# Moving two token mixes of the second batch into the first batch's tail, and its attention front to earlier places in the first FFN

## The chip, the cores and the metric

One core of a Trainium2 chip runs the kernel. The metric is the device time of one execution in microseconds (us), as the median of several runs. The engines are TensorE (PE in the profile, with its weight loads as PEld), VectorE (DVE), ScalarE (ACT), GpSimd (POOL) and SyncE (SP), which issues the DMAs.

## The reference

The input holds 8 batches of 512 tokens. Three layers follow one another; the last two add to their input.

```python
h = jnp.einsum('bhid,oi,od->bho', x, weighted_sum, weight)       # token mix, 1024 -> 256
h = h + attention(layernorm(h))    # qkv, rotate, unit q and k, 16 heads of 16, softmax, out projection
h = h + ffn(layernorm(h))
# ffn: 8 experts, 256 -> 1024 -> 256
w = sigmoid(x @ Wg + bg); w = w * (w > 0.5)
out = sum_e w[:, e] * (relu(x @ W1[e] + b1[e]) @ W2[e] + b2[e])
```

## The kernel before

Each batch has four tiles of 128 tokens. The kernel overlaps the FFN of batch i with the attention of batch i+1. The order is written out as a list of stages, which every engine walks in the same sequence, each doing its own part of a stage and waiting on semaphores. `attention_order` gives every stage a due time, counted in chunks of the FFN; `bodies` merges them with the FFN's stages. There are 64 chunks (8 experts x 8); chunk c has a first matmul `f1 c` (6 matmuls of 512 columns) and, three chunks later, a second `f2 c` (12 matmuls of 256 columns), and after each eighth `f2` comes `acc e`, in which VectorE adds the expert's result to the output tile.

There are four orders: the first (attention of batch 0 alone, then `f1 0` to `f1 3`), the second (FFN of batch 0 beside attention of batch 1), the merged one (six times), and the last. Only the first two are touched here. The stages of an attention are:

- `split t`: ScalarE rounds tile t of the input to its high part (`xh`), and VectorE subtracts for the low part (`xl`), each in two halves.
- `mix t`: TensorE makes the token mix in 24 matmuls of 256 columns (12 for each half of the input), VectorE copies the result to `resid` and takes its statistics (`bn_stats`).
- `ln1`: a chain of small VectorE instructions for the inverse root, then the four normalised tiles.
- `ln1_turn t`, `qkv t`, `rotate t`: transposes, the projection (12 matmuls), then VectorE's work on the rotary part. Then `qk_norm`, `unit t`, `stack t` (ScalarE high part, VectorE low part of q and k), and SP's DMA transposes.
- `scores`, `weigh`, `out_copy`, `out_turn`, and then the tail: `att_turn t`, `project t`, `ln2`, `ln2_turn t`, `logits t`, `gates`, `gates_turn`, `bias2`.

During the second order, the weights of the experts 2 to 7 are also prepared: `maxima 2e` and `maxima 2e+1` search the raw W1 and W2 of expert e on VectorE (one reduction of 128x2048 each), `share e` is a tiny matmul that spreads the maxima over the partitions, `scales e` makes the factors, and `parts 4e` to `parts 4e+3` split the weights (ScalarE high, VectorE low). SP loads the next raw W1 once parts 4e+1 is done, and the next raw W2 once parts 4e+3 is done. So `load_raw` of expert 4 waits for the parts of expert 3.

In the second order GpSimd makes the low part of each hidden chunk (`hl`), and `f2 c` waits for it. The TensorE stage `f1 n` waits for ScalarE's two activations of chunk n-2, since the two banks `bank_h` alternate. The relevant waits in the code are:

```python
elif stage == "f1":                       # TensorE
    wait(pe, h_hi, fb, 2 * (n - 1))
elif stage == "f2":
    wait(pe, h_lo, fb, n + 1)
    ...
        if m == 0 and t % 2 == 0:
            wait(pe, acc_done, fb, TT * (e - 1) + t + 2)
```

Before the change the first order ends with `ln2, ln2_turn, logits, gates, split_ahead 0, f1 0, f1 1, f1 2, gates_turn 0, f1 3, bias2 0`, and the second order opens with `maxima 5, f2 0, split 1, mix 0, f1 4, split 2, mix 1, share 2, f2 1, scales 2, f1 5, split 3, mix 2, f2 2, f1 6, mix 3, f2 3, ln1, f1 7, f2 4, ln1_turn 0, f1 8`. `maxima 4` stands between `scores 28` and `scores 29` of the first order.

## Time and profile before

| | us |
|---|---|
| median of 3 runs | 1892.27 (1889.27 to 1893.55) |
| the profiled execution | 1891.92 |
| its span in the trace | 1890.1 |
| TensorE busy in the span | 1813.9 |
| VectorE busy | 1312.3 |
| ScalarE busy | 1076.7 |

The trace has no marks by batch; by the bias adds of `bias2` (at 128.57 and 370.39 us) the first order ends at about 128.5 us and the second some 10 us after 370. Times below are microseconds from the span's start. A row of the timeline gives start, duration, engine, line, operation and operands; square brackets at its end give the idle time of the engine just before it and who ended that. TensorE's matmul records overlap, so a matmul's pace is the distance between starts and not its duration.

### The profile page before, as it was taken

The numbers are of one execution on the slowest core, as the hardware profiler recorded it, in microseconds if no ns is written. First come the engines' busy times: TensorE is split into PE (matmuls) and PEld (weight loads), VectorE is DVE, ScalarE is ACT, GpSimd is POOL, SyncE is SP. The second block draws the span as 40 slices with busy tenths as digits, with TensorE's granted clock in tenths as the row PEclk, the third lists the DMA queues.
The fourth block names the chain that finished last, engine by engine and source line by source line (L and its number), as shares of the span: only waits on it lengthen the run. The fifth ranks groups of instructions, "written<-read, shape, count | busy, mean of one in ns | idle before, by whom it ended". The sixth has DMA issues, their size and how long they took to land.

```text
span 1890.1 us, 33337 instructions
## 1 busy us (share of the span) xinstructions
PE 1813.9 (96%) x13036; PEld 1173.0 (62%) x13036; DVE 1312.3 (69%) x2469; ACT 1076.7 (57%) x1658; POOL 111.6 (6%) x92
## 2 busy tenths in 40 slices
PE   5689899999999999999999999999999999999999
PEld 4157445775567655776557755677556775566666
DVE  7868645688865888558875788758886588863333
ACT  3745777446654566446664466544765456654444
POOL 1013323200000000000000000000000000000000
PEclk9789999999999999999999999999999999999999
DMA  4332552415122331234312242221512323223221
GB/s 166 112 112 90 147 180 99 168 51 151 69 89 101 84 140 68 69 121 113 112 68 90 79 134 90 89 98 71 156 68 70 121 70 111 89 72 117 92 104 42
DMA packets 103979, 192.40 MB, mean 102 GB/s; under 512 B 67448, under 2 KB 80656, under 8 KB 87440
## 3 DMA queue, kind: packets, MB, share of 16 engines
q1 hardware_dynamic: 103824, 190.28, 30.5%
q8 instruction: 104, 1.70, 0.4%
q14 instruction: 51, 0.42, 0.1%
HBM read 153.55 MB, written 20.97 MB: 92 GB/s over the span
## 4 chain that ended last, share of the span: by engine, by line
PE 81%; DVE 5%; issue 3%; ACT 3%; DMA 2%; DVEq 0%; ACTq 0%; SPq 0%
PE bank_h L1069 32%; PE bank_f L1088 11%; PE bank_f L1090 10%; PE bank_f L1091 10%; PE bank_o L975 4%; PE bank_s L950 4%; PE bank_s L855 3%; PE bank_s L856 3%; PE bank_s L857 3%; DMA qt<-probs 2%; ACT hh L832 1%; PE bank_m L987 1%; PE bank_s L1023 1%; PE bank_m L864 1%; PE bank_o L864 1%
## 5 line engine op out<-in xcount | busy, mean ns | idle before, releaser
L1069 PE MATMUL bank_h<-x,w1s 128*128 128x512 f16 x3072 | 749.7, 381 | 2.4 <-ACT hh L832 2.4
L829 ACT ACTIVATE h<-bank_h,b1s 128x512 f32<-128x512 f32 x512 | 352.2, 688 | 539.9 <-PE bank_h L1069 470.3
L1088 PE MATMUL bank_f<-w2s,hh 128*128 128x256 f16 x2048 | 560.2, 274 | 6.0 <-DVE acc L1362 5.9
L1090 PE MATMUL bank_f<-w2s,hh 128*128 128x256 f16 x2048 | 558.4, 273 | 0.0
L1091 PE MATMUL bank_f<-w2s,hl 128*128 128x256 f16 x2048 | 558.3, 273 | 0.0
L1069 PEld LDWEIGHTS bank_h<-x,w1s 128*128 128x128 f16 x3072 | 289.3, 99 | 296.2 <-issue 23.2
L1144 DVE TENSOR_TENSOR hl<-h,hh 128x512 f16<-128x512 f32 x448 | 309.9, 695 | 136.6 <-PE bank_f L1091 107.0
L832 ACT ACTIVATE hh<-bank_h,b1s 128x512 f16<-128x512 f32 x512 | 349.7, 683 | 0.0
L1088 PEld LDWEIGHTS bank_f<-w2s,hh 128*128 128x128 f16 x2048 | 201.3, 98 | 106.9 <-issue 48.0
L1090 PEld LDWEIGHTS bank_f<-w2s,hh 128*128 128x128 f16 x2048 | 200.6, 98 | 49.7 <-issue 0.3
L1091 PEld LDWEIGHTS bank_f<-w2s,hl 128*128 128x128 f16 x2048 | 200.4, 98 | 23.3
L798 ACT ACTIVATE qk<-bank_s 128x1024 f32<-128x1024 f32 x132 | 135.3, 1025 | 64.3 <-PE bank_s L950 64.2
L1283 DVE TENSOR_TENSOR probs<-qk,probs 128x1024 f16<-128x1024 f32 x132 | 161.8, 1225 | 4.5
L1362 DVE SCALAR_TENSOR_TENSOR acc<-bank_f,gw,acc 128x256 f32<-128x256 f32 x256 | 106.1, 477 | 38.1 <-PE bank_f L1091 37.1
L1282 DVE CAST probs<-qk 128x1024 f16<-128x1024 f32 x132 | 91.1, 690 | 51.9 <-ACT qk L798 51.8
L975 PE MATMUL bank_o<-probs,v 128*32 128x512 f16 (+1 forms) x1408 | 115.3, 427 | 1.0 <-ACT tmp_b L727 0.6
L950 PE MATMUL bank_s<-qt,kt 64*128 64x512 f16 x480 | 94.2, 389 | 15.8 <-DMA qt<-w1s 4.7
L707 POOL TENSOR_TENSOR resid<-resid,outb 128x1024 f32<-128x1024 f32 x8 | 25.4, 3170 | 1135.2 <-DVE normed L1195 1128.5
L680 POOL TENSOR_TENSOR hl<-h,hh 128x512 f16<-128x512 f32 x64 | 76.6, 1196 | 198.5 <-ACT hh L832 148.4
L855 PE MATMUL bank_s<-mix,xh 128*128 128x256 f32 x240 | 73.0, 304 | 14.1 <-DVE xl L1135 12.6
L950 PEld LDWEIGHTS bank_s<-qt,kt 64*128 64x128 f16 x480 | 23.1, 92 | 98.3 <-issue 58.3
L798 ACT ACTIVATE stack<-bank_s 128x1024 f32<-128x1024 f32 x60 | 61.5, 1026 | 37.1 <-PE bank_s L950 37.1
(215 smaller groups left out, 1800.2 us busy)
## 6 DMA issues: line engine op xcount, KB each, us to landing
w1s<-w_parts SPq DMA_DIRECT2D x56, 1024.0 KB, 4.8
w2s<-w_parts SPq DMA_DIRECT2D x56, 1024.0 KB, 4.8
raw<-in_w_dram SPq DMA_DIRECT2D x16, 1024.0 KB, 6.3
xraw<-in_x_t_dram SPq DMA_DIRECT2D x30, 512.0 KB, 6.1
w_parts<-w1s SPq DMA_DIRECT2D x8, 1024.0 KB, 8.8
w_parts<-w2s SPq DMA_DIRECT2D x8, 1024.0 KB, 10.6
out_dram<-acc SPq DMA_DIRECT2D x16, 256.0 KB, 6.0
w1s<-in_x_t_dram SPq DMA_DIRECT2D x2, 512.0 KB, 9.0
```

Source lines behind the costliest of these rows:

```text
L798: act.activation(terms, score_banks(n, fb is None)[:, :, :], ACT.Exp, scale=SCORE_SCALE)\
L829: act.activation(h32[n % 2][:], bank_h[n % 2][:, :], ACT.Relu, bias=b1s[:, e, m:m + 1]).then_inc(h_hi.sem, 1)
L832: act.activation(hh[n % HBUFS][:], bank_h[n % 2][:, :], ACT.Relu, bias=b1s[:, e, m:m + 1]).then_inc(h_hi.sem, 1)
L855: pe.matmul(out_ap, high[k], w[k], start=start and k == 0, stop=False, skip_group_check=True)
L950: pe.matmul(score_banks(n, fb is None)[:, j, :], kt[lo:lo + 64, h // 2, tile * P:(tile + 1) * P], qt[lo:lo + 64, h // 2, :], start=True, s ...
L975: last = pe.matmul(bank_o[32 * j:32 * j + 32, :], v[:, 4 * g + j].rearrange("p s d -> p (s d)"), p[:, j, :], start=(tile == 0 and k == 0), ...
L1069: last = pe.matmul(bank_h[n % 2][:, :], w[:, wp, k, m * P:(m + 1) * P], x16s[fb % 2][:, xp, k, :], start=(k == 0 and wp + xp == 0), stop=( ...
L1088: pe.matmul(o, high, w[:, 0, m, :], start=(m == 0 and t % 2 == 0), stop=False, skip_group_check=True)
L1090: pe.matmul(o, high, w[:, 1, m, :], start=False, stop=False, skip_group_check=True)
L1091: last = pe.matmul(o, low, w[:, 0, m, :], start=False, stop=(m == HM - 1), skip_group_check=True)
L1144: dve.tensor_tensor(hl[n % HBUFS][:], h32[n % 2][:], hh[n % HBUFS][:], ALU.subtract)\
L1283: dve.tensor_tensor(low, exps[n % 3], high, ALU.subtract).then_inc(halved.sem, 1)
```

## The change

Stages of the second batch move, and some change their engine or bank:

- `maxima 4` leaves the scores of the first order and stands at the head of the second.
- `split_ahead 0` (tile 0 of batch 1) goes from just ahead of `f1 0` up to just ahead of `weigh 15`.
- `mix_early 0` to `3` are the two tile mixes 0 and 1 in half tiles of 12 matmuls, in `bank_h` in place of `bank_s`. The first stands between `out_turn 3` and `att_turn 0`, the second between `att_turn 1` and `project 0`, the third and fourth between `project 3` and `ln2`.
- `split_early 0`, `1` split tile 1, the low part on GpSimd in place of VectorE. `resid_early` copies the mix on ScalarE in place of VectorE, and `stats_early` takes its statistics on VectorE, among the `ln2_turn` stages.
- `split_ahead 2` stands where `split_ahead 0` stood.
- In the second order `mix 2` now comes ahead of `f2 0`, and `mix 3` after `f2 1`; `ln1` after `f1 5`, `ln1_turn 0` after `f2 2`. All later stages of the front come sooner: `qkv 0` before `f2 4` (was before `f2 6`), `qk_norm` before `f1 13` (was before `f2 11`), `unit 0` before `f2 12` (was after `f2 14`), `stack 3` before `f2 15` and `acc 1` (was before `f2 17`, after `acc 1`). `share 3` moves from ahead of `f2 13` to behind `acc 1`. From `f2 17` (`scales 3`) on the order is the same as before.

```diff
--- before.py
+++ after.py
@@ -61,8 +61,8 @@
 
     steps = []
     later = not alone and not first_ffn
-    sooner, att_at = (1.5, FIRST_ATT) if first_ffn else (0.0, range(TT))
-    mix, unit = (FIRST_MIX, [u - 0.6 * sooner for u in UNIT]) if first_ffn else (LATER_MIX, LATER_UNIT)
+    sooner, att_at = (3.1, FIRST_ATT) if first_ffn else (0.0, range(TT))
+    mix, unit = (FIRST_MIX, [u - sooner for u in UNIT]) if first_ffn else (LATER_MIX, LATER_UNIT)
     turn, gap, norm = (LATER_TURN, LATER_GAP, LATER_NORM) if later else (9.0 - sooner, 1.5, 15.7 - sooner)
     for t in range(TT):
         steps += [(turn + gap * t, "ln1_turn", t),
@@ -96,12 +96,16 @@
     steps += [(tail + 5.2, "ln2", 0), (tail + 11.2, "gates", 0), (tail + 12.7, "gates_turn", 0),
               (tail + 13.7, "bias2", 0)]
     if alone:
-        steps.append((tail + 12.0, "split_ahead", 0))
+        steps += [(first + pace * 31.5, "split_ahead", 0), (tail + 1.06, "split_early", 0), (tail + 2.05, "split_early", 1),
+                  (first + pace * 35 + 0.3, "mix_early", 0), (tail + 1.05, "mix_early", 1),
+                  (tail + 4.2, "mix_early", 2), (tail + 4.25, "mix_early", 3),
+                  (tail + 3.05, "resid_early", 0), (tail + 5.3, "resid_early", 1),
+                  (tail + 8.45, "stats_early", 0), (tail + 9.25, "stats_early", 1), (tail + 12.0, "split_ahead", 2)]
     else:
 
         steps += [(tail + 3.0, "split_ahead", 0), (tail + 5.3, "mix_ahead", 0), (tail + 5.25, "split_ahead", 1),
                   (tail + 6.4, "mix_ahead", 1), (tail + 12.0, "split_ahead", 2)]
-        here = range(TT // 2 if later else 0, TT)
+        here = range(TT // 2, TT)
         steps += [(mix[t], "mix", t) for t in here] + [(mix[t - 1] - 0.05, "split", t) for t in here[1:]]
     steps.sort(key=lambda s: s[0])
     return steps
@@ -112,7 +116,7 @@
 LATER_TURN, LATER_GAP, LATER_NORM = 4.6, 1.45, 11.0
 LATER_UNIT = [12.8, 14.1, 15.4, 16.7]
 LATER_FIRST, LATER_PACE = 20.2, 0.82
-FIRST_MIX = [3.6, 4.3, 5.2, 6.3]
+FIRST_MIX = [None, None, 3.2, 4.6]
 FIRST_ATT = [0.0, 1.7, 2.5, 3.4]
 UNIT = [18.55, 19.4, 20.2, 21.0]
 PIECES = 4
@@ -128,8 +132,8 @@
     prep = [(63.0, "v_scaled", 0)]
     for e in range(2, EXPERTS):
         start = HM * (e - 1)
-        at = {2: (None, -7.5, -3.55, -3.5, 0.2, 0.9, 3.2, 3.9),
-              3: (-3.8, -1.85, 0.2, 4.5, 4.7, 5.3, 5.9, 6.5),
+        at = {2: (-7.6, -7.5, -3.55, -3.5, 0.2, 0.9, 3.2, 3.9),
+              3: (-3.8, -1.85, 2.9, 4.5, 4.7, 5.3, 5.9, 6.5),
               6: (0.6, 2.0, 3.2, 3.5, 4.3, 5.0, 5.7, 6.4)}.get(e, (0.6, 2.0, 3.7, 3.9, 4.4, 5.0, 5.7, 6.4))
         stages = [("maxima", 2 * e), ("maxima", 2 * e + 1), ("share", e), ("scales", e)]
         stages += [("parts", PIECES * e + p) for p in range(PIECES)]
@@ -158,9 +162,9 @@
     between = {("scores", 0): [("v_max", 0), ("maxima", 0), ("maxima", 1), ("reduce", 0), ("scales", 0),
                                ("parts", 0), ("parts", 1), ("parts", 2), ("parts", 3)],
                ("scores", 12): [("maxima", 2), ("maxima", 3), ("reduce", 1), ("scales", 1), ("parts", 4), ("parts", 5)],
-               ("scores", 20): [("parts", 6), ("parts", 7)], ("scores", 28): [("maxima", 4)],
+               ("scores", 20): [("parts", 6), ("parts", 7)],
                ("scores", 10): [("stack_b2", 0)],
-               ("split_ahead", 0): [("f1", 0), ("f1", 1), ("f1", 2)],
+               ("split_ahead", 2): [("f1", 0), ("f1", 1), ("f1", 2)],
                ("gates_turn", 0): [("f1", 3)]}
     first = []
     for step in attention_order(alone=True):
@@ -679,6 +683,14 @@
                     wait(pool, f2_done, fb, n - HBUFS + 1)
                     pool.tensor_tensor(hl[n % HBUFS][:], h32[n % 2][:], hh[n % HBUFS][:], ALU.subtract)\
                         .then_inc(h_lo.sem, 1)
+                elif stage == "split_early":
+                    high, low = x_parts(1, 1, n)
+                    wait(pool, x_lo, 1, 2 + n)
+                    wait(pool, x_hi, 1, 2 + n + 1)
+                    x_landed(pool, 1, 1)
+                    x_free(pool, 1, 1, n)
+                    pool.tensor_tensor(low, x_rows(1, 1)[:, half_x[n]], high.bitcast(F32), ALU.subtract)\
+                        .then_inc(x_lo.sem, 1)
                 elif stage == "projections" and n == 1:
                     for t in range(TT):
                         wait(pool, v_out, ab, t + 1)
@@ -752,6 +764,12 @@
                         copy(qkvw[:, 0, :, 0:2 * D], qk[:, 0:DK, :]).then_inc(set_hi, 1)
                     else:
                         copy(outw[:, 0].rearrange("p k n -> p (k n)"), raw_out).then_inc(set_hi, 1)
+                elif stage == "split_early":
+                    split_x(1, 1, [n])
+                elif stage == "resid_early":
+                    wait(act, x_used, 1, 2 * (n + 1))
+                    wait(act, h2_out, 0, n + 1)
+                    copy(resid[:, n, :], bank_h[n][:, 0:D]).then_inc(resid_out.sem, 1)
                 elif stage == "mix" and fb is None:
                     wait(act, x_used, ab, 2 * (n + 1))
                     copy(resid[:, n, :], bank_s[n % 2][:, 0:D]).then_inc(resid_out.sem, 1)
@@ -858,6 +876,15 @@
                                      skip_group_check=True)
                 return last
 
+            def mix_half(at, b, t, half):
+
+                wait(pe, x_hi, b, 2 * t + half + 1)
+                wait(pe, x_lo, b, 2 * t + half + 1)
+                ks = range(XK)[half_x[half]]
+                high, low = ([part[:, k % (XK // 2), :] for k in ks] for part in x_parts(b, t, half))
+                parts(at[:, 0:D], high, low, [mix[:, 0, k, :] for k in ks], [mix[:, 1, k, :] for k in ks],
+                      start=half == 0, stop=half == 1).then_inc(x_used.sem, 1)
+
             def turn(signal_, t, source):
 
                 for k in range(DK):
@@ -874,19 +901,16 @@
                     wait(pe, resid_out, ab, n - 1)
                     if ab > 1 and n < 2:
                         wait(pe, h2_out, ab, 0)
-                    elif ab == 1 and n < 2 or ab > 1:
+                    elif ab:
                         wait(pe, accn_ready, ab, 0)
                     for half in range(2):
                         if n == 0 and fb is None:
                             pe.wait_ge(set_lo, half + 1)
-                        wait(pe, x_hi, ab, 2 * n + half + 1)
-                        wait(pe, x_lo, ab, 2 * n + half + 1)
-                        ks = range(XK)[half_x[half]]
-                        high, low = x_parts(ab, n, half)
-                        last = parts(bank_s[n % 2][:, 0:D], [high[:, k % (XK // 2), :] for k in ks], [low[:, k % (XK // 2), :] for k in ks],
-                                     [mix[:, 0, k, :] for k in ks], [mix[:, 1, k, :] for k in ks],
-                                     start=half == 0, stop=half == 1)
-                        last.then_inc(x_used.sem, 1)
+                        mix_half(bank_s[n % 2], ab, n, half)
+                elif stage == "mix_early":
+                    if n == 0:
+                        wait(pe, exped, 0, 2 * UNITS)
+                    mix_half(bank_h[n // 2], 1, n // 2, n % 2)
                 elif stage == "ln1_turn":
                     wait(pe, ln1_out, ab, n + 1)
 
@@ -1055,6 +1079,8 @@
                             last.then_inc(b2_done.sem, 1)
                 elif stage == "f1":
                     e, m = divmod(n, HM)
+                    if fb == 0 and n < 2:
+                        wait(pe, resid_out, 1, n + 1)
                     if n == 0:
                         wait(pe, ln2_lo, fb, TT)
                     if m == 0 and fb == 0:
@@ -1153,6 +1179,10 @@
                     split_x(ab, n, range(2))
                 elif stage == "split_half":
                     split_x(ab, 0, [n])
+                elif stage == "stats_early":
+                    wait(dve, resid_out, 1, n + 1)
+                    dve.bn_stats(mixed_stats[:, n].rearrange("p h s -> p (h s)"), resid[:, n, :])\
+                       .then_inc(mixed_out.sem, 1)
                 elif stage in ("split_ahead", "mix_ahead"):
                     if ab + 1 < BATCHES:
                         steps(stage[:-6], n, fb, ab + 1)
```

## Rows read from the trace of the kernel before

**Rows 1.** The page: busy time by engine, and the chain that ended last, by engine

```profile
PE 1813.9 (96%) x13036; PEld 1173.0 (62%) x13036; DVE 1312.3 (69%) x2469; ACT 1076.7 (57%) x1658; POOL 111.6 (6%) x92
...
PE 81%; DVE 5%; issue 3%; ACT 3%; DMA 2%; DVEq 0%; ACTq 0%; SPq 0%
```

**Rows 2.** Windows of the tail: width, busy by engine, PEclk, DMA share, GB/s

```profile
110.00:115.00 5.00, 0.85 (x6) 0.61 (x6) 4.15 (x22) 0.00 (x0) 0.00 (x0) 0.89 0.06 23
115.00:120.00 5.00, 4.95 (x25) 4.51 (x24) 2.23 (x6) 2.53 (x8) 0.00 (x0) 0.50 0.00 0
120.00:125.00 5.00, 5.00 (x15) 1.82 (x14) 2.66 (x10) 2.81 (x6) 1.04 (x1) 0.59 0.16 39
```

**Rows 3.** Timeline of the tail, TensorE and VectorE

```profile
104.39 0.44 PE L864 MATMUL bank_m<-ident,normed 128*128 128x128 f32 x2 [0.81 <-DVE normed L1290]
...
105.80 0.36 PE L855 MATMUL bank_s<-outw,turned_h 128*128 128x256 f32 x1 [0.76 <-ACT turned_h L727]
...
114.61 0.69 PE L864 MATMUL bank_m<-ident,normed 128*128 128x128 f32 x2 [4.15 <-DVE normed L1315]
...
119.85 6.14 PE L1069 MATMUL bank_h<-x,w1s 128*128 128x512 f16 x18
```

**Rows 4.** Timeline of TensorE: mix 0 and the chunk behind it

```profile
130.07 0.35 PE L855 MATMUL bank_s<-mix,xh 128*128 128x256 f32 x1
...
133.01 1.47 PE L1069 MATMUL bank_h<-x,w1s 128*128 128x512 f16 x6
```

**Rows 5.** Timeline of VectorE: bias add, mix 3, its norm, first rotate, first unit, scales 3

```profile
128.57 1.29 DVE L1348 TENSOR_TENSOR acc<-bank_s,acc 128x512 f32<-128x512 f32 x2 [5.44 <-PE bank_s L1052]
...
148.49 0.43 DVE L1186 COPY resid<-bank_s 128x256 f32<-128x256 f32 x1 [3.45 <-PE bank_s L857]
...
156.53 2.48 DVE L1390 SCALAR_TENSOR_TENSOR w1s<-raw,scl,w1s 128x1024 f16<-128x1024 f32 x2 [2.03 <-ACT w1s L844]
...
159.34 0.68 DVE L1221 TENSOR_TENSOR qk<-bank_s,qkvb 128x512 f32<-128x512 f32 x1
...
187.90 2.26 DVE L1268 TENSOR_TENSOR probs<-qk,y 128x512 f32<-128x512 f32 x2
...
200.53 0.15 DVE L1434 COPY mxr<-bank_m 128x3 f32<-128x3 f32 x1
```

**Rows 6.** Timeline of TensorE: first ln1 transpose, and every later wait up to 221 us but scores

```profile
152.42 0.44 PE L864 MATMUL bank_m<-ident,normed 128*128 128x128 f32 x2
...
193.45 0.27 PE L1088 MATMUL bank_f<-w2s,hh 128*128 128x256 f16 x1 [1.30 <-DVE acc L1362]
...
204.60 1.47 PE L1069 MATMUL bank_h<-x,w1s 128*128 128x512 f16 x6 [1.81 <-ACT hh L832]
207.92 1.46 PE L1069 MATMUL bank_h<-x,w1s 128*128 128x512 f16 x6 [0.54 <-ACT hh L832]
...
220.50 0.27 PE L1088 MATMUL bank_f<-w2s,hh 128*128 128x256 f16 x1 [1.42 <-DVE acc L1362]
```

**Rows 7.** Window from acc 0 to scales 3, columns as in rows 2

```profile
162.86:200.53 37.67, 36.37 (x245) 25.62 (x244) 36.73 (x61) 21.39 (x36) 13.89 (x11) 1.00 0.40 119
```

**Rows 8.** Chain that ended last: start, us, what

```profile
133.17 1.31 PE bank_h L1069 x6
...
210.22 6.77 DMA raw<-in_w_dram
```

**Rows 9.** Timeline of VectorE and GpSimd in qk_norm

```profile
185.42 0.29 DVE L1110 SCALAR_TENSOR_TENSOR y<-y 128x128 f32<-128x128 f32 x1
185.58 1.16 POOL L680 TENSOR_TENSOR hl<-h,hh 128x512 f16<-128x512 f32 x1 [1.45 <-ACT hh L832]
185.74 1.14 DVE L1111 SCALAR_TENSOR_TENSOR y<-y 128x128 f32<-128x128 f32 x1
```

**Rows 10.** Windows behind a TensorE gap at 330 us, columns as in rows 2

```profile
329.00:331.00 2.00, 0.61 (x6) 0.30 (x4) 2.00 (x4) 1.91 (x3) 1.05 (x1) 1.00 0.00 0
...
333.00:335.00 2.00, 2.00 (x7) 0.84 (x6) 1.86 (x10) 0.05 (x1) 0.00 (x0) 0.50 0.36 152
```

## The prediction, on record before the change was built

> **What bounds the kernel now.** I read the page first: TensorE is busy for 1813.9 of 1890.1 us and carries 81% of the chain that ended last [rows 1]. So a change must take work off TensorE, or close one of its few gaps. Both exist around this change. The windows of the tail show the first gap: TensorE does 0.85 us of work in 110 to 115, and its granted clock goes to 0.50 (the 1.2 GHz level) in 115 to 120 and 0.59 in 120 to 125 [rows 2]. The timeline names it: a wait of 4.15 us for the norm [rows 3]. From 128.5 us on TensorE is full, and the mixes lie in it back to back with the chunks [rows 4]. The waits that follow are four: 1.30 (acc 1), 1.81 and 0.54 (the hidden activations, held up behind scales 3 and the parts), 1.42 (acc 2) [rows 6]. They come from VectorE: between acc 0 and scales 3 it is busy for 36.73 of 37.67 us [rows 7], and behind that the chain runs over the raw weights of expert 4, a DMA of 6.77 us [rows 8]. So this stretch has two bounds almost level: TensorE's work and VectorE's order.
>
> **The sum is made against the profiled execution**, 1891.92 us, which is 0.35 under the median.
>
> **Part 1, the tail.** The 12 matmuls of a half mix cost half of what mix 0 took: 133.01 - 130.07 = 2.94 for 24, so 1.47 [rows 4]. The first half mix starts when out_turn 3's transposes are issued (about 103.5) and ends at about 105.0, where the first att_turn transpose started at 104.39 [rows 3]: 0.6 late. The second lies ahead of project 0, from about 105.5 to 107.0, where project 0 started at 105.80 [rows 3]. Everything behind it, the adds, statistics and norm, moves by 1.2. The splits of tile 0 fill idle time of ScalarE and VectorE ahead of out_copy 3 and out_turn 3 (the searches of maxima 4 left VectorE there), so they cost nothing; if that room were not there they would cost ScalarE's 1.2. Half mixes 3 and 4 (2.94) lie in the old gap of 4.15, behind which 4.15 - 2.94 = 1.2 stay idle. GpSimd's two subtractions are nowhere in the trace; the nearest row is its subtraction into f16 of the same 512 elements, 1.16 [rows 9]. They have over 2 us each, so between nothing and twice that row they hide. The ScalarE copies and the two statistics (0.43 each, taking the mix 3 copy as their like [rows 5]) fall into gaps of ln2_turn, up to 0.3 of it on the path to f1 0. The input tiles 2 and 3 are now issued by SP as soon as tiles 0 and 1 are split (about 103 and 111), behind the stores of expert 1 already on the queue, and needed at about 120 and 130. Both wait only for splits of the tail, so SP's next item, raw W1 of expert 3, which needs parts 9, is not held.
>
> What comes back is clock. Under the half clock stand transposes and logits from 114.61, and three f1 chunks in 6.14 from 119.85 [rows 3], which at the full-clock pace of 1.31 a chunk [rows 8] would be 3.9. With the full clock throughout, 2.2 return on the f1 chunks. On the 5.2 from 114.61 to 119.85 between nothing (ScalarE sets the pace) and half, 2.6, returns; I take 1.5, the middle, as the records show TensorE busy but ScalarE between each pair. Tail: -3.7 + 1.2 = -2.5. But a gap needs not be long: at 329 to 331 TensorE still did 0.61 us and by 333 the clock was 0.50 [rows 10]. The new tail has an idle 1.2 and then 3 to 4 us of thin work (transposes and matmuls of 8 columns) behind it. I take it as the likelier that the clock falls there, some 3 us later than before, and is down during the f1 chunks: then about half of the 1.5 returns and, with the chunks starting where they did, perhaps 0.5 at the end of the cold stretch, against 1.2 paid. Tail: 0.
>
> By the Trainium skill (TensorE: Matmul & The Clock Gate, What's actually happening) idleness throttles the clock and sustained activity releases it; filling most of the gap would by that rule alone keep it at 2.4 GHz, and that is the second rival. Rows 10 speak against being sure of it.
>
> **Part 2, the second order up to f1 24.** Times here count from the end of bias2's matmuls, 128.53 before.
> - Removed from TensorE: two tile mixes, 2 x 2.94 = -5.9.
> - Mix 2 now stands ahead of f2 0 and waits for the bias add, which is 1.29 long [rows 5]; before, f2 0 hid it. +1.4.
> - ln1: from VectorE's copy of mix 3 (148.49 [rows 5]) to the first transpose (152.42 [rows 6]) is 3.9; before, f2 3, f1 7, f2 4 lay between, now only f1 5 and f2 2 (2.6). +1.5, for no other work of VectorE remains in front of it.
> - VectorE's long chain. Its start, the bias add of qkv 0, was at 159.34 [rows 5], 30.8 after bias2. By the new order TensorE ends qkv 0 at about 22.3: waits 1.4 + 1.5, mixes 2 and 3 5.9, f2 0 to 3 and f1 4 to 7 8 x 1.31 = 10.5, two transposes and share 2 0.7, qkv 0 with 4608 columns against a mix's 6144, 2.94 x 0.75 = 2.2. It is 8.5 sooner. Unit 0 began at 187.90 (59.4); new ahead of it are the low parts 8 and 9 (2.48 [rows 5]) and some 2.3 of waits for ScalarE and TensorE where VectorE had a backlog before: 59.4 - 8.5 + 2.5 + 2.3 = 55.7. From unit 0 to scales 3 (200.53) it was 12.6, of which I expect 1.3 not to return (one collision as in rival 3, some waiting): scales 3 at 67.0, 5 sooner than its 72.0.
> - acc 1 now stands behind all units and stacks, right ahead of scales 3, so its first two adds end at about 66.1. Before, f2 16 began at 193.45 [rows 6], which is 64.9. TensorE gets to f2 16 at 64.9 - 1.3 - 5.9 + 1.4 + 1.5 = 60.6 and waits.
> - stack 0 stands ahead of f1 16's activation on ScalarE, and needs unit 0, done at about 56.2; with the stack's two copies and the chunk's two activations, 2.4, f1 18 can start at 58.6, where TensorE would be there at 56.9: +1.7. This wait and the next are one behind the other: TensorE now gets to f2 16 at 62.3 to 62.5, waits +3.6 and starts at 66.1, 1.2 later than before.
> - Then the old 1.81 + 0.54 go, since scales 3 is done before the parts need it: f1 24 starts 1.2 sooner. f2 24's 1.42 goes too, because the raw W2 of expert 4 (210.22 [rows 8]) is then issued about 3.5 sooner and its search and acc 2 with it: f2 24 is 2.6 to 2.9 sooner.
> - An idle 3.6 ahead of f2 16 will cost clock: the half clock behind 330 us came after less [rows 10], and while it lasts each chunk pair of 2.6 takes 5.2. I set 0.9, between 0 (the fall lies within the wait) and 1.8 (3.6 us of work at half speed).
>
> Sum: -2.8 + 0.9 = -1.9, and the tail 0: 1890.0 for this execution, **1890.3 as a median**. Maxima 4 (2.28 on VectorE, the same reduction as maxima 5 behind it) is now in the second order while TensorE has mix 2, f2 0 and f1 4 (5.6) ahead of share 2; two searches need 4.4, so it hides; without that cover it would cost share 2 up to 2.2. Behind f2 24 the orders are the same and TensorE is the bound, so what is won stays, up to the clock dip at 333, which may fall otherwise (1.2 either way).
>
> **Rivals.**
> 1. *The tail keeps its clock.* For it: the mixes fill 70% of the gap. Against: thin work and rows 10. Time 1890.3 - 2.5 = 1887.8, and where the dip behind f2 16 is also missing, 1887. With VectorE's chain 1 us better too, 1886.
> 2. *VectorE's order pays it all back.* The stretch between acc 0 and scales 3 is full [rows 7]; if its waits are 4.3 instead of 2.3, f2 16 starts 2 later, and nothing is won: 1892, no change.
> 3. *Slower: collisions in VectorE's chain ahead of acc 1.* A VectorE instruction of 0.29 took 1.14 while GpSimd ran its subtraction [rows 9], and two unit instructions took 2.26 [rows 5]. GpSimd makes one subtraction a chunk, and the front now has VectorE instructions beside chunks where it used to idle. Each further collision puts f2 16 0.85 later. Three beyond the old number eat the 2 us won; seven make it slower by 0.2%, or six if the clock costs 1.8 instead of 0.9. With four to seven it gives 1893 to 1896. The Trainium skill (SBUF — State Buffer, Who interferes with whom) says that such a VectorE instruction with two SBUF inputs and a GpSimd one that reads block each other fully; the trace agrees with its 1.14 beside 1.16. By that rule the count of collisions, not VectorE's work, decides here.
> 4. *The waits are smaller than reckoned.* If ln1, unit and acc fit, the second order gains the whole 5.9 less 1.4, plus old waits, minus what VectorE bounds: about -5, so 1887.
>
> **How the numbers follow.** 0.2% is 3.8 us, about what a measurement can tell from no change. The forecast has 0.43 (its own range 1888.5 to 1892), rival 1 0.22, rival 2 0.13, rival 3 0.10, rival 4 0.12. Faster by over 0.2% are rival 4, most of rival 1 and the best edge of the forecast: 0.33. Slower by over 0.2% is a part of rival 3 with something I don't see: 0.12. Same: 0.55. The range reaches from rivals 1 and 4 together with the dip at 333 gone (1884.5) to rival 3 (1895).
>
> **What the changed profile would show.** First att_turn transpose at about 105.0 and project 0 at 107.0; TensorE busy in the old gap; the granted clock between 115 and 125 decides rival 1. A wait of 1.3 to 1.4 ahead of mix 2, of 1.5 ahead of the first ln1 transpose, of 1 to 2 ahead of f1 18 and of 2 to 5 ahead of f2 16; no wait for the activations at f1 23. The prediction is wrong if f2 16 has no wait (then rival 4), or if project 0 starts where it did.

## The result: 4.6 us slower, and the profile after

| | before | after |
|---|---|---|
| median, us | 1892.34 (1889.27 to 1894.05, 13 runs) | 1896.96 (1895.31 to 1899.11, 13 runs) |
| profiled execution, its span | 1891.92, 1890.1 | 1896.79, 1894.9 |

The ratio is 1.0022, with a 95% interval of 1.0015 to 1.0029. I had forecast 1890.3 with a range of 1884.5 to 1895.0. All ratios here leave out two slow executions, whose mean granted clock was lower than the 0.99 of the others: one of e1_old_front (2088 us at 0.85) and one of the kernel before (1931 us at 0.94).

The page of the changed kernel, busy time and chain by engine, stands against [rows 1]:

```profile
PE 1817.4 (96%) x13036; PEld 1174.3 (62%) x13036; DVE 1312.1 (69%) x2465; ACT 1075.8 (57%) x1660; POOL 114.5 (6%) x94
...
PE 82%; DVE 7%; ACT 5%; issue 4%; DMA 3%; SPq 0%; DVEq 0%; ACTq 0%
```

TensorE makes the same 13036 matmuls and is busy 3.5 us longer, and VectorE's share of the chain rose from 5% to 7%. The first says that matmuls ran slower, the second that TensorE waits more for VectorE. The timeline of TensorE shows every wait between 114 and 222 us except those inside scores (against [rows 3, 6]):

```profile
114.47 0.44 PE L891 MATMUL bank_m<-ident,normed 128*128 128x128 f32 x2 [1.28 <-DVE normed L1345]
...
128.97 0.36 PE L873 MATMUL bank_s<-mix,xh 128*128 128x256 f32 x1 [1.54 <-issue]
...
145.46 0.44 PE L891 MATMUL bank_m<-ident,normed 128*128 128x128 f32 x2 [2.33 <-DVE normed L1225]
...
190.48 2.42 PE L1095 MATMUL bank_h<-x,w1s 128*128 128x512 f16 x6 [2.45 <-ACT hh L850]
...
200.14 0.27 PE L1114 MATMUL bank_f<-w2s,hh 128*128 128x256 f16 x1 [3.77 <-DVE acc L1392]
```

The old wait of 4.15 is 1.28. The four later waits of before (1.30, 1.81, 0.54, 1.42) are gone, and four others came: ahead of mix 2, of the first ln1 transpose, of f1 18 and of f2 16, together 10.1 against 5.1.

Windows of the changed kernel, columns as in rows 2 (the granted clock is the third number from the end):

```profile
115.00:120.00 5.00, 4.85 (x25) 4.07 (x24) 3.12 (x10) 2.91 (x10) 0.00 (x0) 0.58 0.00 0
120.00:125.00 5.00, 5.00 (x20) 2.13 (x19) 2.30 (x9) 3.44 (x7) 1.19 (x2) 0.74 0.00 0
125.00:130.00 5.00, 3.38 (x19) 2.21 (x18) 2.54 (x4) 2.90 (x5) 3.43 (x3) 0.94 0.00 0
130.00:135.00 5.00, 5.00 (x33) 4.69 (x33) 4.54 (x5) 1.26 (x2) 0.00 (x0) 0.72 0.02 3
...
145.00:150.00 5.00, 4.54 (x20) 2.74 (x21) 1.77 (x5) 1.65 (x3) 0.85 (x1) 0.66 0.00 0
190.00:195.00 5.00, 4.52 (x21) 2.64 (x22) 4.69 (x6) 5.00 (x10) 3.00 (x3) 0.66 0.75 144
195.00:200.00 5.00, 1.37 (x7) 0.40 (x5) 4.96 (x8) 2.12 (x4) 2.60 (x2) 1.00 0.88 169
200.00:205.00 5.00, 4.86 (x23) 2.72 (x24) 2.14 (x11) 0.32 (x1) 0.00 (x0) 0.66 0.94 110
```

Behind each of the four waits the clock falls to its 1.2 GHz level and comes back within 5 us. A mean of 0.66 over 5 us loses 0.34 x 5 = 1.7 us of work; 0.72 loses 1.4, and with the 0.3 of the 0.94 ahead of it 1.7 again. The f1 chunk at 190.48 takes 2.42 where one takes 1.47 at full clock. In the trace of before every window from 125 to 225 us is at 1.00, its waits of 1.30 to 1.81 and all ([rows 7] is one of them).

**Where the time went.** The bias add behind each `bias2` marks the ends of the orders. In the timeline of VectorE of the changed kernel the marks and the main stations of the second order are (against [rows 5]):

```profile
127.46 1.29 DVE L1378 TENSOR_TENSOR acc<-bank_s,acc 128x512 f32<-128x512 f32 x2 [5.03 <-PE bank_s L1076]
...
143.22 1.14 DVE L1137 SCALAR_TENSOR_TENSOR y<-y 128x4 f32<-128x4 f32 x1
...
153.84 0.69 DVE L1251 TENSOR_TENSOR qk<-bank_s,qkvb 128x512 f32<-128x512 f32 x1 [0.34 <-PE bank_s L875]
...
187.41 1.28 DVE L1298 TENSOR_TENSOR probs<-qk,y 128x512 f32<-128x512 f32 x2
...
191.04 2.06 DVE L1306 TENSOR_TENSOR probs<-probs 128x512 f16<-128x512 f32 x2
193.21 1.46 DVE L1298 TENSOR_TENSOR probs<-qk,y 128x512 f32<-128x512 f32 x1
...
197.97 1.12 DVE L1385 TENSOR_SCALAR gw<-gw,unscale 128x4 f32<-128x4 f32 x1
...
200.70 0.15 DVE L1464 COPY mxr<-bank_m 128x3 f32<-128x3 f32 x1
...
372.73 1.29 DVE L1378 TENSOR_TENSOR acc<-bank_s,acc 128x512 f32<-128x512 f32 x2
```

From bias add to bias add the second order took 370.39 - 128.57 = 241.82 before and 372.73 - 127.46 = 245.27 after: +3.45. The first order ended 1.11 sooner. The last pair of bias adds of the run came at 1715.5 before and 1720.3 after, 4.8 later, so another 2.5 arose in the six merged orders, whose code is the same: 0.8 in the first of them, and 1.8 in the fifth, where the changed kernel has a clock fall at 1344 us that before does not have. That part differs between executions; the runs below say what is known of it.

### The profile page after: what moved, and what is told of

Its sections match the earlier page's. It is cut to its first block, busy times and chain, and to the rows that moved or that the text cites. A ratio compares the mean times of both kernels' runs of the same rounds, so it can differ in the third digit from the quotient of the medians.

```text
span 1894.9 us, 33339 instructions
## 1 busy us (share of the span) xinstructions
PE 1817.4 (96%) x13036; PEld 1174.3 (62%) x13036; DVE 1312.1 (69%) x2465; ACT 1075.8 (57%) x1660; POOL 114.5 (6%) x94
## 4 chain that ended last, share of the span: by engine, by line
PE 82%; DVE 7%; ACT 5%; issue 4%; DMA 3%; SPq 0%; DVEq 0%; ACTq 0%
PE bank_h L1095 31%; PE bank_f L1114 11%; PE bank_f L1117 10%; PE bank_f L1116 10%; PE bank_o L999 5%; PE bank_s L974 4%; PE bank_s L873 3%; PE bank_s L875 3%; PE bank_s L874 3%; DMA qt<-probs 2%; ACT probs L816 1%; ACT hh L850 1%; PE bank_m L1011 1%; PE bank_s L1047 1%; DVE qk L1251 1%
## 5 line engine op out<-in xcount | busy, mean ns | idle before, releaser
L974 PEld LDWEIGHTS bank_s<-qt,kt 64*128 64x128 f16 x480 | 23.2, 93 | 98.1 <-issue 58.7
L873 PE MATMUL bank_s<-mix,xh 128*128 128x256 f32 x224 | 68.6, 306 | 15.5 <-DVE xl L1161 12.4
```

Source lines behind the costliest of these rows:

```text
L873: pe.matmul(out_ap, high[k], w[k], start=start and k == 0, stop=False, skip_group_check=True)
L974: pe.matmul(score_banks(n, fb is None)[:, j, :], kt[lo:lo + 64, h // 2, tile * P:(tile + 1) * P], qt[lo:lo + 64, h // 2, :], start=True, s ...
```

## The experiments

The small table gives all runs in one place: the median, its distance from and ratio to the kernel before, which was measured again beside each group of runs, and the length of the second order (the distance between those two bias adds in the profiled execution). The medians of before beside them were 1891.4 to 1892.4, so a difference between the medians of two groups can be off by 1.

| run | median | less before | ratio (95%) | second order |
|---|---|---|---|---|
| before | 1892.34 | 0 | 1 | 241.82 |
| after | 1896.96 | +4.6 | 1.0022 (1.0015 to 1.0029) | 245.27 |
| e1_old_front | 1888.5 | -3.6 | 0.9985 (0.9976 to 0.9994) | - |
| e12_old_front_again | 1890.17 | -1.7 | 0.9986 (0.9977 to 0.9996) | 239.03 |
| e2_mix2_behind_f2 | 1894.83 | +2.7 | 1.0013 (1.0004 to 1.0021) | 242.61 |
| e3_units_late | 1891.99 | -0.1 | 0.9999 (0.9991 to 1.0008) | 241.08 |
| e5_mix2_and_units | 1890.05 | -2.4 | 0.9990 (0.9981 to 0.9998) | 238.44 |
| e6_front_between | 1885.23 | -7.2 | 0.9963 (0.9950 to 0.9975) | 234.41 |
| e8_before_units_sooner | 1895.79 | +3.4 | 1.0020 (1.0011 to 1.0029) | 245.16 |
| e7_maxima_back | 1896.85 | +4.4 | 1.0028 (1.0017 to 1.0038) | 245.27 |
| e4_filled_waits | 1901.67 | +9.6 | 1.0059 (1.0047 to 1.0072) | 244.66 |
| e10_two_fills | 1895.78 | +4.4 | 1.0025 (1.0015 to 1.0035) | 242.12 |
| e11_fill_elsewhere | 1904.4 | +13.0 | 1.0071 (1.0057 to 1.0085) | 245.64 |
| e9_tail_filled | 1888.35 | -3.0 | 0.9982 (0.9973 to 0.9991) | 236.09 |

### e1_old_front: the tail as changed, the front where it stood

```diff
-    sooner, att_at = (3.1, FIRST_ATT) if first_ffn ...
-    mix, unit = (FIRST_MIX, [u - sooner for u in UNIT]) ...
+    sooner, att_at = (1.5, FIRST_ATT) if first_ffn ...
+    mix, unit = (FIRST_MIX, [u - 0.9 for u in UNIT]) ...
-FIRST_MIX = [None, None, 3.2, 4.6]
+FIRST_MIX = [None, None, 5.2, 6.3]
-              3: (-3.8, -1.85, 2.9, ...
+              3: (-3.8, -1.85, 0.2, ...
```

> The tail as changed, but every later stage of the front (mix 2, mix 3, ln1, qkv, units, stacks, share 3) back at its old due time. Two tile mixes less for TensorE in the second order. If the loss comes from the sooner front (waits and the falls of the clock behind them), the loss goes and part of the 5.9 us of mixes is won: 1889 to 1891. If the tail itself costs (its half mixes ahead of project 0), it stays above 1894.

The median is 1888.5, 0.15% under before and 8.5 under after. Taking the mixes out of the second order is worth time; what loses is the place of the front. Its profiled execution is the one of 2088 us, so its trace is not read; e12 is the same kernel again, and has one.

### e2_mix2_behind_f2 and e3_units_late: the two moves inside the front, one at a time

```diff
# e2
-FIRST_MIX = [None, None, 3.2, 4.6]
+FIRST_MIX = [None, None, 3.6, 4.6]
# e3
-    mix, unit = (FIRST_MIX, [u - sooner for u in UNIT]) ...
+    mix, unit = (FIRST_MIX, [u - 0.9 for u in UNIT]) ...
```

> Only mix 2 goes behind f2 0, which then covers the bias add. Clock theory: the wait of 1.54 us and the fall of the clock behind it both go, 2.5 to 3 us in all, 1894 to 1894.5. VectorE-order theory: the vector engine's chain up to acc 1 decides and starts hardly sooner, so under 1 us: 1896 to 1897.

> Only units and stacks go back to their old due times, so acc 1 stands ahead of unit 2 again. VectorE-order theory: the waits of 2.45 us (f1 18) and 3.77 us (f2 16) shrink to about 1.5 together, and the cold stretches behind them go: 1892 to 1893. Clock theory of the early waits alone (mix 2, ln1): these stay, so no better than 1895.

With f2 0 ahead of mix 2 the kernel is 2.1 faster than after (2.7 in the second order): the wait of 1.54 is gone with the clock fall behind it. With the units at their old places it is 5.0 faster (4.2 in the second order). The timeline of TensorE and one window of e3 show what remains of the two late waits:

```profile
193.99 0.27 PE L1114 MATMUL bank_f<-w2s,hh 128*128 128x256 f16 x1 [0.89 <-DVE acc L1392]
...
205.56 2.44 PE L1095 MATMUL bank_h<-x,w1s 128*128 128x512 f16 x6 [2.23 <-ACT hh L850]
...
205.00:210.00 5.00, 4.44 (x19) 2.50 (x20) 3.35 (x4) 5.00 (x7) 2.35 (x2) 0.66 0.60 117
```

f2 16 starts 65.5 us behind the start of its bias add (128.53) and waits 0.89, where after had 72.7 and 3.77. The price of the old places is the 2.23 ahead of f1 23 with a clock fall behind it (the chunk takes 2.44, the window has 0.66), less than what they save.

### e4_filled_waits: idle time filled with matmuls

```diff
+FILL = {('mix', 2): 6, ('ln1_turn', 0): 9, ('f1', 18): 8, ('f2', 16): 14}
+            def warm(count):
+                for _ in range(count):
+                    pe.matmul(bank_o[:, :], x16s[0][:, 0, 0, 0:P], x16s[0][:, 0, 0, :], start=True, stop=True, ...)
```

> The changed kernel with 37 more matmuls of 512 columns on data that is there, into a bank that nobody reads, at the four waits (6 ahead of mix 2, 9 ahead of ln1_turn 0, 8 ahead of f1 18, 14 ahead of f2 16: 8.0 us at full clock into 10.1 us of waits). Their results are not used. Clock theory: the granted clock stays at 1.00 from 125 to 210 us and 4 to 6 us come back: 1891 to 1893. Order theory: TensorE's clock does not matter while VectorE is the bound, under 1.5 us: 1895.5 to 1897.

The forecast for the whole run failed: it is slower than after by 4.7. Up to chunk 51 of the first FFN it runs 3.1 ahead of the changed kernel (counted from the same start); all of it is won by chunk 7, behind the first two fills, where the clock now stays at 1.00, as the clock theory says. The third and fourth won nothing, since VectorE bounds that part: f2 16 still waits 2.49, and the clock still falls behind it (0.66 from 195 to 200 us). Of the 3.1, 2.5 are lost again by the end of the order, around a clock fall at 333 us that the changed kernel does not have, and from 370 us on to the last bias add the run is 6.9 longer than after. This led to e10 and e11.

### e5_mix2_and_units: e2 and e3 together

> The changed kernel with both repairs: mix 2 behind f2 0, units and stacks at their old due times. If they repair different things (the clock behind the bias wait; the vector engine's order ahead of acc 1), their gains of 2.1 and 5.0 us add: 1889.5 to 1890.5. If the first only shifts work to where the second would have waited anyway, it stays at 1891.5 or more.

The edits are those of e2 and e3. 1890.05 is 6.9 under after, against 2.1 + 5.0 = 7.1 apart: the two moves add up. It still waits 2.33 ahead of the first ln1 transpose. It also has nearly the wait of e3 ahead of f1 23, but here the clock does not fall:

```profile
202.18 1.47 PE L1095 MATMUL bank_h<-x,w1s 128*128 128x512 f16 x6 [2.22 <-ACT hh L850]
...
200.00:205.00 5.00, 2.78 (x18) 1.68 (x18) 3.09 (x3) 5.00 (x7) 1.16 (x1) 1.00 0.67 129
```

The order of the stages around that wait is the same in both. So whether the clock falls behind a wait of 2.2 is not decided by its length and its neighbours alone.

### e6_front_between: a place between

```diff
-    sooner, att_at = (3.1, FIRST_ATT) if first_ffn ...
-    mix, unit = (FIRST_MIX, [u - sooner for u in UNIT]) ...
+    sooner, att_at = (2.1, FIRST_ATT) if first_ffn ...
+    mix, unit = (FIRST_MIX, [u - 0.9 for u in UNIT]) ...
-FIRST_MIX = [None, None, 3.2, 4.6]
+FIRST_MIX = [None, None, 3.6, 4.9]
```

> As the run before, and the transposes and qkv one chunk later than in the change, so that ln1's chain of about 4 us is covered by four blocks of TensorE work. No wait ahead of mix 2 or of ln1_turn 0, so the clock stays up. Clock theory: another 2.5 us or more against the run before, 1887 to 1888.5. If these waits cost only themselves and VectorE bounds the stretch anyway: equal to the run with the old front, 1888.5.

1885.23 (5 runs) is 7.1 under before and 11.7 under after, 1.8 better than the range of the forecast. All waits of TensorE from its bias2 to 221 us, but scores, in the timeline of e6:

```profile
185.35 0.27 PE L1114 MATMUL bank_f<-w2s,hh 128*128 128x256 f16 x1 [1.27 <-DVE acc L1392]
...
196.53 1.47 PE L1095 MATMUL bank_h<-x,w1s 128*128 128x512 f16 x6 [1.84 <-ACT hh L850]
...
199.85 1.46 PE L1095 MATMUL bank_h<-x,w1s 128*128 128x512 f16 x6 [0.54 <-ACT hh L850]
...
212.44 0.27 PE L1114 MATMUL bank_f<-w2s,hh 128*128 128x256 f16 x1 [1.43 <-DVE acc L1392]
```

and two of its windows, where the changed kernel has 0.72 and 0.66:

```profile
130.00:135.00 5.00, 5.00 (x40) 3.99 (x39) 4.91 (x9) 2.04 (x4) 1.16 (x1) 1.00 0.02 3
...
145.00:150.00 5.00, 5.00 (x34) 3.87 (x33) 1.66 (x3) 2.58 (x4) 2.07 (x2) 1.00 0.01 3
```

The waits ahead of mix 2 and ln1 are gone, those of before are back ([rows 6], nearly to the hundredth), and none of them drops the clock. The second order is 7.4 shorter than before's: the 5.9 of the two mixes, and 1.5 that fit the clock fall behind 330 us [rows 10], which this run does not have. This is the fastest version.

### e7_maxima_back: maxima 4 back among the first order's scores

```diff
-        at = {2: (-7.6, -7.5, ...
+        at = {2: (None, -7.5, ...
+               ("scores", 28): [("maxima", 4)],
```

> The changed kernel with maxima 4 back among the scores of the first order. If its new place costs nothing (covered by mix 2, f2 0, f1 4), within 1 us of the changed kernel: 1896 to 1898. If the searches hold up the split of tile 3 and the vector chain, 2 us faster: 1895.

1896.85 against 1896.96, and 245.27 for the second order in both: its new place costs nothing in this kernel.

### e8_before_units_sooner: the units sooner in the kernel before

```diff
-    mix, unit = (FIRST_MIX, [u - 0.6 * sooner for u in UNIT]) ...
+    mix, unit = (FIRST_MIX, [u - 3.1 for u in UNIT]) ...
```

> The kernel before with units and stacks alone 2.2 chunks sooner, so that stack 0 stands ahead of the activation of chunk 16 and all units ahead of acc 1. VectorE-order theory: the stalls ahead of f1 18 and f2 16 appear here too, with nothing given in return: 1895 to 1898. If the order is harmless and only the change's other waits hurt: within 1.5 us of 1892.

This one move makes the old kernel 3.4 slower (3.3 in the second order). The timeline of TensorE of e8:

```profile
190.05 1.47 PE L1069 MATMUL bank_h<-x,w1s 128*128 128x512 f16 x6 [1.89 <-ACT hh L832]
...
199.77 0.37 PE L1088 MATMUL bank_f<-w2s,hh 128*128 128x256 f16 x1 [5.64 <-DVE acc L1362]
```

f2 16 starts 6.3 later than before (193.45, [rows 6]) because all units and stacks now lie on VectorE ahead of acc 1; part is given back by the later waits, which go. Around its start the clock falls once (0.91 and 0.75 in the windows from 195 to 205 us), which it does not in the kernel before.

### e10_two_fills and e11_fill_elsewhere: the fills that win, and a control

```diff
# e10
+FILL = {('mix', 2): 6, ('ln1_turn', 0): 9}
# e11, in the first order, where TensorE is idle for 10 us
+FILL = {('key_turn', 0): 37}
```

> The changed kernel with fills at the two early waits alone, 6 ahead of mix 2 and 9 ahead of ln1_turn 0, results not used. Clock theory: up to chunk 51 of the first FFN it gains what the run with four fills gained there, about 3 us, since the two later fills stood where VectorE was the bound. What the whole run gives depends on the waits ahead of scores 0 of the later batches: with the changed kernel's (8.7 us) 1894, with those of the run with four fills (12.3 us) 1899 to 1901.

> A control: the changed kernel with 37 more matmuls of the same size where TensorE is idle for 10 us anyway, ahead of key_turn 0 of the first batch; results not used. If a longer TensorE program alone lengthens the waits ahead of scores 0 of the later batches, it shows them at 12 us and is at 1900 or more, as the run with four fills. If it does not: 1896 to 1898, with 8 to 9 us of these waits.

e10's second order is 3.15 shorter than the changed kernel's, and the bias add of qkv 0 comes 3.2 sooner, 23.2 behind the first bias add. Its windows:

```profile
130.00:135.00 5.00, 5.00 (x40) 4.23 (x40) 5.00 (x5) 1.26 (x2) 0.00 (x0) 1.00 0.02 3
145.00:150.00 5.00, 5.00 (x31) 3.42 (x30) 0.82 (x3) 2.75 (x5) 1.15 (x1) 1.00 0.00 0
```

Nothing but those 15 matmuls is different, and the waits they fill would else be idle, so 3.1 is what the two clock falls cost. Next to nothing of it reaches the median: e10 is 4.4 above the kernel before beside it, and after was 4.6 above its own. The control says where such a gain goes: e11 adds its matmuls where nobody waits for them, and is 13.0 above before, 8.4 worse than after. Its second order is only 0.4 longer. The waits by releaser of the changed kernel, and then of e11 (engine, tile, line, who ended it: us, times, longest):

```profile
PE bank_s L974 <- issue: 4.7, 4, 1.5
...
PE bank_s L974 <- DMA qt<-probs: 4.0, 2, 2.3
```

```profile
PE bank_s L983 <- issue: 8.8, 4, 2.9
...
PE bank_s L983 <- DMA qt<-probs: 4.1, 2, 2.1
```

These are the six waits ahead of scores 0 of the later batches, where the code lets TensorE wait for the DMA transposes of q and k; the profile names the DMA at two of them and nobody ("issue") at the others. Together they grow from 8.7 to 12.9 (12.3 in e4, 10.3 in e10). The windows of e11 show clock falls near 670, 1120, 1350 and 1580 us, each directly behind one of these waits, where after has one, at 1344. The 4.2 of waits and three more falls at 1.7 are 9.3 of the 9.5 by which e11's profiled execution is longer. So the fills bear a cost of their own, hundreds of microseconds behind them; the loss of e4's total says nothing against the clock theory. Here too the length of a wait does not settle it: the kernel before waits 2.20 at 1340 us and stays at full clock behind it.

### e9_tail_filled: the tail at full clock

The edit is e6 with 11 matmuls of 512 columns ahead of ln2_turn 0, 2, 3 and logits 2.

```diff
+FILL = {('ln2_turn', 0): 5, ('ln2_turn', 2): 2, ('ln2_turn', 3): 2, ('logits', 2): 2}
```

> The fastest version so far (front between the old and the changed one) with 11 more matmuls of 512 columns in the first batch's tail, 5 in the remaining wait of 1.27 us ahead of ln2_turn 0 and 2 each ahead of ln2_turn 2, ln2_turn 3 and logits 2, on data that is there, into a bank that nobody reads. Their results are not used. If thin work is what lets the clock fall in the tail, it stays at 1.00 from 110 to 125 us and the f1 chunks start and run 1 to 2 us sooner than without: 1883.5 to 1884.5. If the fill delays the transposes as much as it saves: 1885 to 1886.5.

The clock is 1.00 in every window from 110 to 125, and f1 0 to 2 take 4.28 in place of 5.73. Counted from out_turn 3's transposes the tail wins 0.7 (24.56 to the bias add in e6, 23.85 here), since f1 0 starts 0.7 later behind the fills. The second order is 1.7 longer than e6's, all of it at one clock fall near 325 us. The windows from 115, first e6 and then e9:

```profile
115.00:120.00 5.00, 4.67 (x27) 3.24 (x28) 4.14 (x16) 3.44 (x11) 0.00 (x0) 0.85 0.00 0
120.00:125.00 5.00, 5.00 (x22) 2.16 (x21) 0.84 (x2) 3.84 (x7) 2.31 (x2) 0.80 0.00 0
```

```profile
115.00:120.00 5.00, 4.82 (x34) 3.50 (x34) 3.51 (x11) 2.99 (x10) 0.00 (x0) 1.00 0.00 0
```

The total, forecast at 1883.5 to 1884.5, is 3.1 slower than e6, with 10.1 of waits ahead of the later scores 0 where e6 has 8.5, and clock falls at 1335 and 1563 us: the same late cost as in e4, e10 and e11.

### e12_old_front_again: e1 once more

> The first experiment once more, for a profile that can be read: time again 1887.5 to 1889.5. Its front stands where that of the kernel before stood, with two mixes less ahead of it. Expected: no wait ahead of mix 2 and none of 2 us ahead of ln1_turn 0, the clock at 1.00 from 130 to 200 us, and acc 1's wait at 1 to 2 us as before. The 5.9 us of the two mixes come back only in part, since VectorE is the bound from acc 0 to scales 3.

The edit is e1's. The time is 0.7 above the forecast, with nearly the ratio to before of e1. The timeline of TensorE of e12 has a wait that I had not expected:

```profile
133.01 0.59 PE L1062 MATMUL bank_m<-mx,v 128*128 128x3 f32 x2 [3.12 <-DVE mx L1407]
```

That is share 2, waiting for the searches maxima 4 and 5. With mix 2 back behind f2 1 only f2 0 and f1 4 lie ahead of it, and the windows behind, from 130 to 140 us, show the clock at 0.80 and 0.85, one fall. So in this order maxima 4's new place has lost the cover that the prediction named, and costs 3.1 and a clock fall; e1 and e12 understate what the old front is worth: without the two mixes (5.9) and the fall behind 330 us (1.5), with this wait (3.1) and fall (1.7), the second order should be 2.6 under before's, and it is 2.8 under. No run has the old front with maxima 4 at its old place.

## Why the prediction was wrong

**The step that failed is the clock term of part 2: "An idle 3.6 ahead of f2 16 will cost clock ... I set 0.9".** It priced one fall, behind one wait. Four came. I had the waits of mix 2 and ln1 in my own list, at 1.4 and 1.5, and gave them no clock, although the trace showed what a thin stretch does at 330 us [rows 10]. Those two falls cost 3.1 (e10), and because they lie ahead of qkv 0 they delay VectorE's whole chain, on which f2 16 depends. They are the larger part of the miss in the second order, which was forecast at -1.9 and came at +3.45. The rest is VectorE's chain itself: even with the two falls gone (e10) f2 16 starts at 69.5, where I had 66.1.

Point by point, in time from the bias add's start:

- **The tail, "Tail: 0".** Right. From out_turn 3's transposes (102.92 before, 101.93 after) to the bias add it took 25.65 and 25.53. Inside, project 0 starts 0.94 later in that count (1.2 expected), and the clock gives it back: 0.58 and 0.74 against 0.50 and 0.59 [rows 2]. That the first order ended 1.1 sooner was there, but for 0.1, before the first changed matmul, and seven other kernels with this same tail have the bias add anywhere from 126.06 to 128.53. The tail's own length is not fixed either: it is 24.6 in e4, e6 and e12, where the clock is down for a shorter time (0.85 and 0.80 in e6's windows), and 25.5 in the others. So "0" is what this execution shows, and up to 1 us better was as possible. Rival 1 (the tail keeps its clock; the sentence on the Trainium skill calls it the second by mistake) did not come; e9, which forces it with fills, wins 0.7 against e6, not 2.5.
- **Two mixes out of the second order, -5.9.** Right: e6 shows it whole.
- **Waits: 1.4, 1.5, 1.7, 3.6.** They came at 1.54, 2.33, 2.45 and 3.77, and the old ones went. ln1's is 0.85 over because one VectorE instruction of 0.16 took 1.14 at 143.22, beside GpSimd's subtraction at 143.19 (timeline of GpSimd of the changed kernel):

```profile
143.19 1.15 POOL L684 TENSOR_TENSOR hl<-h,hh 128x512 f16<-128x512 f32 x1 [4.46 <-PE bank_f L1117]
...
197.75 1.30 POOL L684 TENSOR_TENSOR hl<-h,hh 128x512 f16<-128x512 f32 x1 [1.46 <-ACT hh L850]
```

- **qkv 0's bias add at 22.3.** It came at 153.84 - 127.46 = 26.4, that is 4.1 late: two clock falls of 1.7 (3.1 by e10) and the 0.85.
- **Unit 0 at 55.7.** It came at 60.0, 4.3 late; the stretch between took 33.6 where I reckoned 33.4. So this stretch was priced well as a whole, with some luck: two of the further collisions lie in it (1.8), and only about 0.7 of the 2.3 of waits that I had reckoned. What was late was its start.
- **Scales 3 at 67.0.** It came at 73.2. From unit 0 it took 13.3 where I had 11.3: I let 1.3 of the old 12.6 not return, and instead it rose by 0.7. The busy time is the same, 13.0 in both: four instructions or groups of them are stretched there, as four were before (2.06, 1.46, 3.45 and 1.12, against 1.28, 0.69, 2.56 and 0.22 undisturbed; 3.3 in sum both times). So the collision that I let go did not go, and the 0.7 is in short gaps between the instructions.
- **f2 16 at 66.1.** It came at 72.7. The 6.6 are 4.1 from the start of the chain, 0.2 in it, 2.0 behind unit 0, and 0.3 because f2 16 starts 0.6 ahead of scales 3 where I had 0.9. The fall behind it cost 1.7, not 0.9. Against this the fall behind 330 us [rows 10] is missing, 1.5 to 1.7 given back. From -1.9 these make -1.9 + 6.6 + 0.8 - 1.7 = +3.8; measured +3.45.
- **Maxima 4, nothing.** Right in this kernel (e7), and the loss without its cover, put at up to 2.2, was 3.1 in e12.
- **"Behind f2 24 ... what is won stays."** Not shown. 2.5 of the 4.8 arose after 370 us in the profiled pair, 1.8 of it in the order with the clock fall at 1344 us. Over 13 runs the difference is 4.6, so something of it stays on average; e11 shows that the later batches do react to changes in the first.

**The rivals.** Rival 3 had the right sign and nearly the size (1893 to 1896). Its mechanism is the smaller half of the truth: from the bias add of qkv 0 to scales 3 seven instructions are stretched by 0.8 to 1.0, 6.0 in sum, where before has four such and one of 0.5, 4.2 in sum, and one more lies in ln1's chain (143.22). That is three or four collisions beyond the old number, the low end of what it named. And e10 has the collisions without the two early falls, and its second order is 242.12, only 0.3 over before's; the falls are the larger half.

**A second term was mis-sized: the balance of the units' early place.** Without it my sum was -5.9 + 1.4 + 1.5 = -3.0, with it -2.8, so I had it at 0.2, and at 1.1 with the clock term. It costs 4.2 in the second order of after (against e3) and 3.3 in that of before (e8), of which up to 1.7 is the one clock fall more that each of the two has. The waits given back, "the old 1.81 + 0.54" and "1.42", were right, 3.8 together; but f2 16 starts 6.3 later in e8 and 7.2 later in after than in e3. I had counted on a chain of VectorE that starts 8.5 sooner to pay for this. It starts 4.4 sooner (26.4 against 30.8), which is mostly the clock falls' doing (7.5 sooner in e10), and the 2.0 behind unit 0 come on top. Rival 2, that VectorE's order pays it all back, was the right place at too low a price. Rival 4 (smaller waits) was wrong: all four were longer than reckoned.

The Trainium skill (TensorE: Matmul & The Clock Gate, What's actually happening) has idleness throttle the clock and sustained activity release it. The runs agree where the waits are 1.5 and 2.3 (0.72 and 0.66, and 1.00 once filled). Left open is the line between a wait that drops it and one that doesn't: e6 waits 1.84 ahead of an f1 chunk and stays at 1.00, the changed kernel waits 1.54 ahead of mix 2 and falls, and ahead of the same f1 23 the clock falls behind 2.23 in e3 and not behind 2.22 in e5.

**What stays open.** Why a longer TensorE program lengthens the waits ahead of scores 0 in later batches (8.7 to 12.9 with 37 matmuls more) was not settled; no run here separates the place of the DMAs from the time of their issue. What decides whether a short wait drops the clock was not found, so a forecast can give such a fall a chance and a price, and not its certainty. Nor was it tried to keep both the early ln1 and a filled wait with real work of the kernel in place of idle matmuls.

## What to carry to other kernels

Price every new wait of TensorE with the clock behind it, the short ones too: behind waits of 1.5 to 2.5 it fell in some places and not in others (e3 and e5), and where it fell about 1.7 us of work were lost. Bringing a front sooner pays only up to where its first stage finds its input ready; past that point each wait on it is also a delay of the long chain behind it. e6 stops just short of that. Work taken out of a stretch is worth its full time (5.9) only if what is left still covers the chains that it covered.

## What the runs showed of the hardware that I had not expected

- The clock fell behind waits of 1.54 and 2.33 in a stretch where TensorE was otherwise at work; 15 matmuls of 512 columns in the two waits kept it at 1.00. Nearly the same wait ahead of the same chunk had the fall in one kernel (2.23, e3) and not in another (2.22, e5).
- 37 matmuls that delay nothing near them made the run 7.4 to 8.4 us longer, nearly all of it in later batches: the bias adds behind the first two orders come 0.2 and 0.6 later than in the changed kernel, and those of four later batches 2.9, 3.8, 7.4 and 9.5.
- A VectorE instruction of 0.16 or 0.22 takes 1.12 to 1.15 beside GpSimd's subtraction of 1.15 to 1.30, also when it handles only four elements a partition (143.22 and 197.97 us).
